# Score tiles of layer A in one pass, with GpSimd folding sums for the all-zero-row test

## The reference

```python
# layer A: 12 heads of 32, residual around it
h = layernorm(x)
scores = einsum('bqhd,bkhd->bhqk', q(h), k(h)) * 384**-0.5 + (adj + adj)[:, None]
row_nonzero = any(scores != 0, axis=-1, keepdims=True)     # the all-zero-row test
p = nan_to_num(softmax(where(row_nonzero, scores, -inf)))  # such a row gives zeros
x = x + (p @ v(h)) @ Wo.T + bo
# layer B: 3 experts of 128, causal mask, residual around it
gate = softmax(relu(h2 @ Wg1 + bg1) @ Wg2 + bg2)           # h2 = layernorm(x)
w = the two largest of the three gates, softmaxed; 0 for the lowest
y_e = softmax(mask(q_e k_e / sqrt(128))) @ v_e             # expert 0: q through a width-3 convolution
x = x + concat(w_e * y_e) @ Wp + bp
```

## Time and profile before

| | us |
|---|---|
| median of 3 runs | 2404.18 (2404.14 to 2409.28) |
| the profiled execution's own time | 2405.69 |
| its span, first to last instruction | 2403.7 |
| TensorE busy | 2250.9 (94%), granted clock 0.99 |
| VectorE busy | 1958.9 (81%) |
| ScalarE busy | 1636.6 (68%) |
| GpSimd busy | 1332.7 (55%) |

### The profile page before, as it was taken

How to read it: one execution, slowest core, us unless ns; L and a number is a source line. 1 busy time by engine, 2 the same in 40 slices (tenths; PEclk the granted TensorE clock), 3 DMA queues, 4 the chain that set the end, 5 groups by cost and what they waited for, 6 DMA issues and landing times.

```text
span 2403.7 us, 52336 instructions
## 1 busy us (share of the span) xinstructions
PE 2250.9 (94%) x16896; PEld 1603.9 (67%) x16896; DVE 1958.9 (81%) x7876; ACT 1636.6 (68%) x5290; POOL 1332.7 (55%) x1193
## 2 busy tenths in 40 slices
PE   2799999999999999999999999999999999999988
PEld 1566777666777666767666777667677667767666
DVE  4788878888888888888888888888888888878884
ACT  2676676676676776666776766776766766766863
POOL 1555664655655655655555655555656555646542
PEclk9899999999999999999999999999999999999999
DMA  5211222211222111222111222112222212222200
GB/s 150 58 51 39 67 71 71 52 51 41 71 71 71 48 48 48 71 72 71 48 42 53 71 71 71 45 41 58 71 71 60 54 40 62 71 71 58 54 18 27
DMA packets 142271, 143.25 MB, mean 60 GB/s; under 512 B 16816, under 2 KB 141360, under 8 KB 142000
## 3 DMA queue, kind: packets, MB, share of 16 engines
q1 hardware_dynamic: 142000, 139.91, 21.5%
HBM read 39.18 MB, written 25.17 MB: 27 GB/s over the span
## 4 chain that ended last, share of the span: by engine, by line
PE 64%; DVE 23%; SPq 4%; issue 4%; DMA 2%; ACT 1%; POOL 1%; DVEq 0%; POOLq 0%; ACTq 0%
PE B_bank L470 23%; PE A_bank L470 22%; PE A_bank L530 5%; DVE S L838 4%; SPq L441 4%; DVE smax L846 3%; PE B_bank L549 3%; PE A_bank L517 3%; DVE sbias L845 2%; PE A_bank L542 2%; DVE V L829 2%; DMA adj<-in_adj 2%; PE B_bank L524 2%; PE B_bank L496 2%; PE B_bank L534 2%
## 5 line engine op out<-in xcount | busy, mean ns | idle before, releaser
L625 ACT ACTIVATE S<-S,sbias,s_unit_neg 128x128 f32<-128x128 f32 x1536 | 736.5, 484 | 191.4 <-DVE smax L846 191.4
L977 POOL TENSOR_TENSOR S<-S,rowf 128x512 f32<-128x512 f32 x384 | 389.4, 1043 | 546.8 <-DVE rowf L865 546.8
L838 DVE CUSTOM_DVE_ANT_0 S<-A_bank,adj 128x128 f32<-128x128 f32 x1536 | 352.0, 284 | 18.6 <-PE A_bank L517 17.9
L982 POOL TENSOR_TENSOR S<-S,row2f 128x384 f32<-128x384 f32 x128 | 106.0, 828 | 353.3 <-DVE row2f L873 353.3
L625 ACT ACTIVATION_READ_ACCUMULATOR S<-S,sbias,s_unit_neg 128x1 f32 x1536 | 294.5, 192 | 0.0
L640 ACT ACTIVATE PT<-A_bank 128x512 f32<-128x512 f32 x384 | 217.3, 593 | 75.8 <-PE A_bank L530 75.8
L846 DVE TENSOR_REDUCE smax<-S 128x4 f32<-128x512 f32 x384 | 260.3, 678 | 0.0
L994 POOL TENSOR_SCALAR h<-x,mv,rstd 128x384 f32<-128x384 f32 x128 | 213.1, 1665 | 27.5 <-POOL rstd L990 27.5
L530 PE MATMUL A_bank<-ident,S 128*128 128x128 f32 x1536 | 217.2, 275 | 7.7 <-DVE V L829 4.5
L944 POOL TENSOR_SCALAR h<-xin,mv,rstd 128x384 f32<-128x384 f32 x126 | 213.2, 1704 | 13.7 <-issue 6.9
L530 PEld LDWEIGHTS A_bank<-ident,S 128*128 128x128 f32 x1536 | 182.7, 142 | 28.0 <-DVE V L829 4.7
(11 more groups left out here) (168 smaller groups left out, 6607.5 us busy)
## 6 DMA issues: line engine op xcount, KB each, us to landing
xin<-in_x SPq DMA_DIRECT2D x32, 768.0 KB, 4.6
Qs<-q_hi SPq DMA_DIRECT2D x256, 96.0 KB, 2.2
Ks<-k_hi SPq DMA_DIRECT2D x256, 96.0 KB, 2.6
out<-x1res SPq DMA_DIRECT2D x128, 192.0 KB, 1.9
Qs<-q_lo SPq DMA_DIRECT2D x128, 96.0 KB, 2.2
Ks<-k_lo SPq DMA_DIRECT2D x128, 96.0 KB, 2.2
adj<-in_adj SPq DMA_DIRECT2D x32, 256.0 KB, 3.5
S<-in_wq SPq DMA_DIRECT2D x1, 576.0 KB, 5.9
```

What stands on the lines that cost most here:

```text
L625: ins = nc.scalar.activation(S[b % 2][:, h, :], S[b % 2][:, h, :], ACT.Exp, bias=sbias[b % 2][:, h:h + 1], scale=s_unit_neg[:], accum_out= ...
L838: ins = nc.vector.tensor_tensor_reduce(S[b % 2][:, h, :], src[:, j * T:(j + 1) * T], adj2[:, b, :], 1.0, 3.0e38, ALU.add, ALU.min, smin[b ...
L977: nc.gpsimd.tensor_tensor(S[b % 2][:, hs, :], S[b % 2][:, hs, :], rowf[b % 2][:, hs].unsqueeze(2).broadcast_to([P, HPC, T]), ALU.mult).the ...
```

## The change

Layer A's score step on VectorE becomes one pass. The instruction that adds the adjacency also multiplies by `s_unit`, so that its minimum is the final one; it writes to a buffer of its own, `raw_score[c]`, one for each c, and its last instruction frees the bank. The instructions for `sbias` and `smax` are gone. ScalarE reads `raw_score[c]`, with the minimum as bias and -1.0 as scale, and writes `S`; it signals after each tile, since VectorE has to wait with the next sequence's tile of the same c until the exponential and the fold below have read the buffer.

The maximum in the all-zero-row test is replaced by a sum over the row, which GpSimd prepares. New steps `A.tree.b.c` add the two halves of each of the four rows (256 outputs a partition); the third one of a sequence also folds all twelve heads' results twice more (to 32, then to 16 columns a head). VectorE sums the last 16 in `A.norm` (`ssize`, twelve rows of 16). The buffer `folded` is one for all sequences, so that every `A.tree.b.c` first waits on the semaphore `sized` for VectorE's `ssize` of sequence b-1.

The norms on GpSimd are written as `(x + (-mean)) * rstd`, with one more tiny instruction for `-mean`, and the scaling of the adjacency as `* adj_unit * 1.0`. The gate has one link fewer: its second exponential takes the gates themselves and not their distance from the largest, so that the largest, that distance and one copy are gone. Bare semaphore increments (`apart`) are removed.

```diff
 ORDER_OF_STEPS, "pool" (the other lists keep their order):
-        A.res A.norm.0 A.ln1 B.res A.norm.1 B.norm.0 B.norm.1 A.norm.2 A.ln2.0 A.norm.3 A.adj
-        B.norm.2 A.ln2.1 B.norm.3 A.ln2.2 A.ln2.3
+        A.res A.tree.0.0 A.tree.0.1 A.tree.0.2 A.norm.0 A.tree.1.0 A.ln1 A.tree.1.1 A.tree.1.2
+        A.tree.2.0 B.res A.tree.2.1 A.norm.1 A.tree.2.2 B.norm.0 A.tree.3.0 A.tree.3.1 B.norm.1
+        A.norm.2 A.tree.3.2 A.ln2.0 A.norm.3 A.adj B.norm.2 A.ln2.1 B.norm.3 A.ln2.2 A.ln2.3
...
 ScalarE, score of A:
-                    for h in range(c * HPC, (c + 1) * HPC):
-                        ins = nc.scalar.activation(S[b % 2][:, h, :], S[b % 2][:, h, :], ACT.Exp,
-                                                   bias=sbias[b % 2][:, h:h + 1], scale=s_unit_neg[:],
+                    for j in range(HPC):
+                        h = c * HPC + j
+                        ins = nc.scalar.activation(S[b % 2][:, h, :], raw_score[c][:, j, :], ACT.Exp,
+                                                   bias=smin[b % 2][:, h:h + 1], scale=-1.0,
                                                    accum_out=ssum[b % 2][:, h:h + 1])
-                    if c == KC - 1:
-                        ins.then_inc(exped, 1)
+                    ins.then_inc(exped, 1)
...
 VectorE, gate part 1:
-                    v.tensor_reduce(gmin[:], over_e(gates), AXX, ALU.min)
-                    link(v.tensor_reduce(gmax[:], over_e(gates), AXX, ALU.max))
-                    v.tensor_tensor(d2[:], gates[:], each_e(gmax), ALU.subtract).then_inc(gate_step, 1)
-                    v.tensor_tensor(above[:], gates[:], each_e(gmin), ALU.not_equal)
+                    link(v.tensor_reduce(gmin[:], over_e(gates), AXX, ALU.min))
+                    v.tensor_tensor(sel[:], gates[:], each_e(gmin), ALU.not_equal)
                     v.tensor_tensor(lowest[:], gates[:], each_e(gmin), ALU.is_equal).then_inc(gate_step, 1)
...
 VectorE, score of A:
                     wait_products(dve, step, g)
-                    apart(dve)
+                    if not (static_zero(g) and b == 0):
+                        dve.wait_ge(exped, count(g, GB * KC, (b - 1) * KC + c + 1))
+                        dve.wait_ge(halved, count(g, GB * KC, (b - 1) * KC + c + 1))
                     for j in range(HPC):
                         h = c * HPC + j
                         ins = nc.vector.tensor_tensor_reduce(
-                            S[b % 2][:, h, :], src[:, j * T:(j + 1) * T], adj2[:, b, :], 1.0, 3.0e38,
+                            raw_score[c][:, j, :], src[:, j * T:(j + 1) * T], adj2[:, b, :], s_unit[:], 3.0e38,
                             ALU.add, ALU.min, smin[b % 2][:, h:h + 1])
-                    ins.then_inc(biased, 1)
-                    dve.wait_ge(biased, count(g, GB * KC, b * KC + c + 1))
-                    hs = slice(c * HPC, (c + 1) * HPC)
-                    nc.vector.tensor_scalar(sbias[b % 2][:, hs], smin[b % 2][:, hs], s_unit[:], None, ALU.mult)
-                    nc.vector.tensor_reduce(smax[b % 2][:, hs], S[b % 2][:, hs, :], AXX, ALU.max).then_inc(freed, 1)
+                    ins.then_inc(freed, 1)
...
 VectorE, norm of A:
+                    wait_evacuated(dve, ("A", "score", b, KC - 1), g)
                     nc.vector.tensor_scalar(live[k][:], smin[k][:], 0.0, None, ALU.not_equal).then_inc(guard, 1)
                     dve.wait_ge(guard, count(g, 2 * GB, 2 * b + 1))
-                    dve.wait_ge(exped, count(g, GB, b + 1))
+                    dve.wait_ge(folded_down, count(g, 2 * GB, 2 * b + 2))
+                    nc.vector.tensor_reduce(ssize[k][:], folded[:, :, 0:T // 8], AXX, ALU.add).then_inc(sized, 1)
+                    dve.wait_ge(exped, count(g, GB * KC, (b + 1) * KC))
                     nc.vector.reciprocal(rinv[k][:], ssum[k][:])
-                    nc.vector.scalar_tensor_tensor(out=live2[k][:], in0=smax[k][:], scalar=0.0, in1=live[k][:],
+                    dve.wait_ge(sized, count(g, GB, b + 1))
+                    nc.vector.scalar_tensor_tensor(out=live2[k][:], in0=ssize[k][:], scalar=0.0, in1=live[k][:],
                                                    op0=ALU.not_equal, op1=ALU.max).then_inc(guard, 1)
...
 GpSimd, norms (the same in ln2):
+                nc.gpsimd.tensor_scalar(nmean1[:], mv1[:, :, 0], -1.0, None, ALU.mult)
-                    ins = nc.gpsimd.tensor_scalar(h1[:, b, :], xin[:, b, :], mv1[:, b, 0:1], rstd1[:, b:b + 1],
-                                                  ALU.subtract, ALU.mult)
+                    ins = nc.gpsimd.tensor_scalar(h1[:, b, :], xin[:, b, :], nmean1[:, b:b + 1], rstd1[:, b:b + 1],
+                                                  ALU.add, ALU.mult)
...
 GpSimd, new:
+                elif kind == "tree":
+                    hs = slice(c * HPC, (c + 1) * HPC)
+                    wait_evacuated(pool, ("A", "score", b, c), g)
+                    if not (static_zero(g) and b == 0):
+                        pool.wait_ge(sized, count(g, GB, b))
+                    nc.gpsimd.tensor_tensor(folded[:, hs, :], raw_score[c][:, :, 0:T // 2],
+                                            raw_score[c][:, :, T // 2:T], ALU.add).then_inc(halved, 1)
+                    if c == KC - 1:
+                        for n in range(2):
+                            w = T >> (n + 2)
+                            if n == 0:
+                                pool.wait_ge(halved, count(g, GB * KC, (b + 1) * KC))
+                            else:
+                                pool.wait_ge(folded_down, count(g, 2 * GB, 2 * b + 1))
+                            nc.gpsimd.tensor_tensor(folded[:, :, 0:w], folded[:, :, 0:w], folded[:, :, w:2 * w],
+                                                    ALU.add).then_inc(folded_down, 1)
```

More of the change, by code:

```diff
@@ L134 @@
 ORDER = {e: parse(text) for e, text in ORDER_OF_STEPS.items()}
-GATE_LINKS = 18
+GATE_LINKS = 17
 def evac_engine(step):
@@ L215, in build @@
         S = [sb(f"S{k}", [P, NH, T]) for k in range(2)]
+        raw_score = [sb(f"raw_score{k}", [P, HPC, T]) for k in range(KC)]
         PT = [sb(f"PT{k}", [P, HPC * T]) for k in range(KC)]
@@ L223, in build @@
         rstd1 = sb("rstd1", [P, GB])
+        nmean1 = sb("nmean1", [P, GB])
         smin = [sb(f"smin{k}", [P, NH]) for k in range(2)]
-        sbias = [sb(f"sbias{k}", [P, NH]) for k in range(2)]
-        smax = [sb(f"smax{k}", [P, NH]) for k in range(2)]
+        ssize = [sb(f"ssize{k}", [P, NH]) for k in range(2)]
+        folded = sb("folded", [P, NH, T // 2])
         ssum = [sb(f"ssum{k}", [P, NH]) for k in range(2)]
@@ L255, in build @@
         g_prod = q2raw[:, 0:NE * GB * GH].rearrange("p (e b n) -> p e b n", e=NE, b=GB)
-        g_tmp = [sb(f"g_tmp{k}", [P, NE, GB]) for k in range(9)]
-        g_col = [sb(f"g_col{k}", [P, GB]) for k in range(7)]
+        g_tmp = [sb(f"g_tmp{k}", [P, NE, GB]) for k in range(7)]
+        g_col = [sb(f"g_col{k}", [P, GB]) for k in range(6)]
         g_w = sb("g_w", [P, NE, GB])
@@ L704, in weight_scales @@
                     link_scale(nc.vector.tensor_scalar(s_unit[:], s_kk[:], A_SCALE / QK_SHIFT ** 2, None, ALU.mult))
-                    link_scale(nc.vector.tensor_scalar(s_unit_neg[:], s_unit[:], -1.0, None, ALU.mult))
                     link_scale(nc.vector.reciprocal(s_kk[:], s_unit[:]))
@@ L748, in gate @@
             def gate(part, g):
-                k = [(0, 6, 12)[part]]
+                k = [(0, 6, 11)[part]]
                 def link(ins):
@@ L986, in do @@
                     pool.wait_ge(moments2, count(g, GB, b + 1))
-                    apart(pool)
+                    nc.gpsimd.tensor_scalar(nmean2[:, b:b + 1], mv2[:, b, 0:1], -1.0, None, ALU.mult)
                     nc.gpsimd.tensor_scalar(ve2[:, b:b + 1], mv2[:, b, 1:2], EPS, None, ALU.add).then_inc(vareps2, 1)
@@ L992, in do @@
                     pool.wait_ge(rstd2_done, count(g, GB, b + 1))
-                    apart(pool)
-                    nc.gpsimd.tensor_scalar(h2[:, b, :], x1[:, b, :], mv2[:, b, 0:1], rstd2[:, b:b + 1],
-                                            ALU.subtract, ALU.mult).then_inc(h2_ready, 1)
+                    nc.gpsimd.tensor_scalar(h2[:, b, :], x1[:, b, :], nmean2[:, b:b + 1], rstd2[:, b:b + 1],
+                                            ALU.add, ALU.mult).then_inc(h2_ready, 1)
                 elif kind == "ln1" and not last:
```

44 lines of the change are left out of this document (17 added, 27 removed).

## The result

The changed kernel takes 2417.88 us (median of 5 runs, 2417.09 to 2421.41), the kernel before 2404.18 (5 runs): a ratio of 1.0055, interval 1.0041 to 1.007. It is slower by 13.7 us. I forecast 2401, no change that can be told; the time lies in the range (2389 to 2442), the direction is the opposite of the forecast's -4.

A forecast was written before the change was run, and what follows sets the result against it. TensorE, busy 94% of the span, was taken as the bound. From 2405.7 us, -4 over 31 passes and -1 (-0.8 for `h` at the start) gave 2400.7, said as 2401; 8-in-10 range 2389 to 2442.

The forecast's parts named there:

- The mechanism: VectorE's burst causes two TensorE waits; these go, but `x1res` behind `ssize` makes `A.turn.1.0` wait some 2.5 us a pass.
- Both waits: TensorE's recurring waits: 47.6 us for the bank before `A.hT.2` and 29.4 us before `B.score.0`, together 77.0 us.
- The failed step: On TensorE, waits before `A.hT.2` and `B.score.0` become one before `A.turn.1.0`, 2.5 us; -4 us over 31 passes.
- The gain of 0.13 us a pass: On TensorE, `A.hT.2` starts at 1170.64 against 1170.77: 0.13 us won a pass, -4 us over 31 passes.
- The gate at nothing: VectorE's gate: the dropped instructions were blocked ones; in the new order another blocks, so nothing was counted.
- rival 1: VectorE's `live` multiply meets `A.tree.2.0`, so `rowf` is held to 1168.46: +0.5 to +0.7 us a pass, 2421; chance 0.22.
- Rival 2: GpSimd's norms keep 1.67 us as add, mult, so pieces of `A.norm.3` come late: 2438 us; chance 0.16.
- Rival 3: TensorE's 77.0 us of waits go, with `x1res` and `A.norm.1` not held behind `sized`: 2329 us; chance 0.13.

The follow-up runs named there:

- ten dummies: Changed kernel with 10 dummy identity transposes on TensorE ahead of the wait of `A.turn.1.0`, order unchanged: 2401.24 us, ratio 0.9983.
- 25 dummies: Changed kernel with 25 dummy identity transposes on TensorE ahead of the wait of `A.turn.1.0`, order unchanged: 2407.75 us, ratio 1.001.
- the first variant: Changed kernel with only `x1res` (`B.res`) moved ahead of `A.tree.2.0` in GpSimd's list: 2314.48 us, ratio 0.9619.

## Why the prediction was wrong, point by point

- *The mechanism was right.* Both waits go, and `A.turn.1.0` waits in every pass for `A.norm.1` behind `x1res`. The forecast pause was 2.5 us; it is 2.83. `x1res` begins 0.84 us after the end of `ssize` (under 1 was forecast), after 6.18 us in which GpSimd had nothing it was allowed to do. Moving `x1res` alone takes it away (2314.48 us).
- *The failed step* is "What was two waits becomes one of 2.5 us. Sum over 31 passes: -0.13 x 31 = -4 us". I priced a pause at its length. Two pauses of 0.94 and 1.58 us left the clock at 2.4 GHz; one of 2.83 brings it to 1.2 GHz for some 3.4 us in 12 passes, at 1.67 us each: +20, where I had none. The variant with ten dummies has the same order and no such fall, and takes 2401.24 us. That this is within 0.3 us of the forecast is in part luck: the next point has two errors, of 7 and 6 us, that cancel.
- *The gain of 0.13 us a pass* was -0.1 instead: 72.30 against 72.20. Two hand-overs account for 0.18 of the difference of 0.23: from the end of `ssize` (1093.09) to the halving 0.15 us where I gave 0.08, and from the end of the first piece (1098.03 + 1.04 = 1099.07) to `A.turn.1.0` 0.16 where I gave 0.05. The 0.23 are worth 7 us over 31 passes; the wait of `B.turn.2`, whose end I had not counted, gave 6 back.
- *Sizes.* Halving 0.73 us forecast, 733 ns measured; folds 1.0 and 0.6, 998 and 599; `ssize` 0.35, 353. `h` 0.83, measured 0.67. The second pointer operand up to 0.07 a head, measured 61 ns (345 against 284). GpSimd's busy time was put at some 58 of 72 us a pass and is 48.9: 41.66 + 15 is 57, and the faster norms, which I did not take off, save 8.
- *The gate at nothing.* In the sum it was in the times already, by the shorter row of instructions. But I did not work out what the row would cost with the old gate left in: 50 us more in this kernel, 30 in the others. Two pieces met instead of one is the same price as in rival 1, and it stands in the trace of before, at L785 and L788.
- *Rival 1 (the lock costs one piece more, 2421)* came nearest in time and is refuted as a mechanism: `rowf` took 0.67 us, ended with the first halving, and `A.hT.2` waits for nothing. What it priced, one piece more by a margin of some 0.01 us, is what eight passes with 25 dummies show, at another instruction, and a piece a pass is what the old gate adds. Its lower end was summed wrong: +0.5 us a pass gives 2421, not 2416.
- *Rival 2 (add, mult no faster)* is refuted by 667 and 669 ns. By the 1.03 cycles an element of the Trainium skill, GPSIMD Engine Reference, "3.1 Elementwise — side-by-side cycle accounting", I had an estimate of 0.33 us plus dispatch. The runs show 0.67 for this form and 1.67 for subtract, mult, two forms of two operations each, which that rule does not tell apart.
- *Rival 3 (both waits go and nothing replaces them, 2329)* is what the variants with `x1res` ahead do, at 2314, better than I had reckoned from the two waits alone. Their spans are 91 us shorter than before: 77 are the two waits, 6 the wait of `B.turn.2`; the rest is covered by TensorE's busy time, 9.4 lower at the same number of instructions (2241.5 in the first variant against 2250.9). Part of that is the clock at the start: from 73 to 92 us the granted clock is 0.73 in that variant and 0.55 in the kernel before. The condition I named for it, that `x1res` isn't held behind `sized`, was the right one.
- *The range and the chances.* 0.40 for slower came from rivals 1 and 2, and neither was the cause.

## What to carry to other kernels

A pause of the engine that bounds the kernel has two prices, its length and what the clock does after it. Here two pauses of 0.94 and 1.58 us left the clock alone, and a single one of 2.31, shorter than both together, did not. When work moves to an idle engine with a queue of its own, look first at what now stands behind the new wait there: here one name in a list was worth 103 us, more than the whole gain over the kernel before. And when a row of small instructions meets another engine's long ones, count the pieces that it is held by: the instruction dropped here saved 0.93 us a pass, not its own 0.16.
